# Experts on tokens sorted by expert: ranks and scatters in self-attention, 39 blocks of 256 rows, results scattered back and added

## What is computed

```python
x = x + xattn(layernorm(x), ctx, ctx, mask)       # 128 batches, 32 queries, 257 keys, 16 heads of 8
x = x + attn(layernorm(x), Wq, bq, ..., Wo, bo)   # causal, 32 tokens a batch, log-distance decay
x = x + ffn(layernorm(x), ...)                    # 8 experts, top 2
# ffn, for 4096 tokens xt of 128 channels:
ew, ei = top_k(xt @ gate_w, 2); ew = softmax(ew)
h = gelu(xt @ w1[e] + b1[e])                      # 128 -> 256
o = h @ w2[e] + b2[e]                             # 256 -> 128
y = norm(xt + o) * ln_g[e] + ln_b[e]
out = sum over the two chosen e of ew[e] * y
```

## Time and profile before

| what | value |
|---|---|
| median of 3 runs | 980.72 us |
| profiled execution, its own time | 979.43 us |
| its span, first to last instruction | 977.7 us |
| PE busy | 828.2 us, 85% |
| DVE busy | 829.6 us, 85% |
| ACT busy | 661.4 us, 68% |
| POOL busy | 448.4 us, 46% |
| mean granted TensorE clock | 0.971 of 2.4 GHz |

### The profile page before, as it was taken

The page is one execution under the profiler, slowest core; times in us unless marked ns, Lnnn a source line. Parts: engine busy times, 40 slices in busy tenths (PEclk is TensorE's granted clock), DMA queues, the critical chain, the costliest instruction groups (busy, mean ns, idle before and its releaser), DMA issues. The chain is left out here.

```text
span 977.7 us, 30213 instructions
## 1 busy us (share of the span) xinstructions
PE 828.2 (85%) x9453; PEld 668.0 (68%) x9453; DVE 829.6 (85%) x2343; ACT 661.4 (68%) x2102; POOL 448.4 (46%) x437
## 2 busy tenths in 40 slices
PE   4989889898889988896788888887989889889892
PEld 2666656666666666664678888887888788788782
DVE  4888889888898988986688887874899999999994
ACT  3677777777677777774676666663777677677674
POOL 3222222222222222221454444443677887787785
PEclk9999999999999999999799998999999999999997
DMA  3221111111111111131000000000000000000000
GB/s 85 75 73 49 48 39 49 36 49 48 36 49 41 46 49 38 49 104 61 1 1 0 0 0 0 0 1 1 1 7 11 5 5 11 5 5 11 5 5 17
DMA packets 32695, 27.26 MB, mean 28 GB/s; under 512 B 3548, under 2 KB 32408, under 8 KB 32664
## 3 DMA queue, kind: packets, MB, share of 16 engines
q1 hardware_dynamic: 32664, 26.87, 9.5%
HBM read 24.76 MB, written 2.10 MB: 27 GB/s over the span
## 5 line engine op out<-in xcount | busy, mean ns | idle before, releaser
L545 ACT ACTIVATE E<-SC,neg_max 128x257 f32<-128x257 f32 x512 | 235.9, 474 | 101.7 <-DVE neg_max L605 101.7
L605 DVE TENSOR_REDUCE neg_max<-SC 128x1 f32<-128x257 f32 x512 | 181.9, 418 | 36.4 <-PE SC L402 33.6
L415 PE MATMUL ETP<-ident,E 128*128 128x128 f32 x1024 | 162.8, 287 | 37.7 <-ACT E L545 37.3
L614 DVE TENSOR_TENSOR Et<-ETP,mask_T 128x512 f32<-128x512 f32 x256 | 172.6, 684 | 15.9 <-PE ETP L415 14.8
L415 PEld LDWEIGHTS ETP<-ident,E 128*128 128x128 f32 x1024 | 109.4, 142 | 88.3 <-issue 78.7
L1337 PE MATMUL PO<-W,hid 128*128 128x128 f32 x1024 | 138.1, 278 | 18.8 <-ACT hid L1378 18.8
L1402 ACT ACTIVATE Y<-Z,zb,zs 128x128 f32<-128x128 f32 x256 | 111.0, 485 | 59.9 <-DVE zb L1557 59.9
L1337 PEld LDWEIGHTS PO<-W,hid 128*128 128x128 f32 x1024 | 131.4, 192 | 29.0 <-issue 21.6
L1326 PE MATMUL PH<-xT,W 128*128 128x256 f32 x512 | 135.1, 387 | 0.5 <-ACT xT L1370 0.5
L1378 ACT ACTIVATE hid<-PH,b1c 128x256 f32<-128x256 f32 x256 | 105.5, 463 | 19.4 <-PE PH L1326 17.8
L545 ACT ACTIVATION_READ_ACCUMULATOR E<-SC,neg_max 128x1 f32 x512 | 103.8, 203 | 0.0
(11 more groups left out here) (163 smaller groups left out, 1551.3 us busy)
## 6 DMA issues: line engine op xcount, KB each, us to landing
V<-in_ctx_dram SPq DMA_DIRECT2D x64, 256.0 KB, 2.7
xh<-in_x_dram SPq DMA_DIRECT2D x32, 64.0 KB, 2.2
last_rep<-in_ctx_dram SPq DMA_DIRECT2D x128, 2.0 KB
X<-in_x_dram SPq DMA_DIRECT2D x32, 64.0 KB
out_dram<-Xo SPq DMA_DIRECT2D x64, 32.0 KB, 1.5
W<-in_L_ffn_w_dram SPq DMA_DIRECT2D x1, 1024.0 KB
W<-in_L_ffn_w_dram SPq DMA_DIRECT2D x2, 512.0 KB
b2r<-in_L_ffn_b_dram SPq DMA_DIRECT2D x1, 512.0 KB
```

Source lines behind the costliest of these rows:

```text
L415: i = pe.transpose(ETP[s][:, c:c + P], E[:, j // HB, NQ * (j % HB) + 2 * s + u, k * P:(k + 1) * P], ident[:, :])
L545: i = act.activation(E[:, h, at, :], SC[:, u, 0:S], ACT.Exp, bias=neg_max[:, j % 2, u:u + 1], accum_out=den[:, h, at:at + 1])
L605: dve.tensor_reduce(neg_max[:, j % 2, u:u + 1], SC[:, u, 0:S], AX.X, ALU.max, negate=True).then_inc(max_sb, 1)
L614: dve.tensor_tensor(Et[:, 2 * (j % 2) + s, :, :, :].rearrange("p u k c -> p (u k c)"), ETP[s][:, :], mask_T[:, :, :, :].rearrange("p u k c ...
```

## The change

Stage 1 also fills a DRAM array "slots" (129 slots of 256 rows of 130 words) with empty rows: weight zero, and a destination outside the result. Stage 2 handles, in body t, also tile t-2 for routing: it normalises the new X into XN (written twice, once for each choice, with room for the weight and the destination), and computes the gates. In every second body from the fourth on it chooses two experts for 512 tokens with masks and maxima, ranks the tokens within each expert by products with a triangle and with ones, and gets each row's place in slots, where every expert has room for 16 blocks. POOL scatters the rows by indirect DMAs of 128 rows, 4 for each tile, from body 5 on. The loops of this stage are written out, T + 3 = 19 bodies. At its end DVE lists the blocks in a table: for each of 39, its slot and its expert. Stage 3 runs 39 blocks; SP reads slot and expert from the table and loads rows and first-layer weights; PE, ACT and DVE read the expert into a register each. The weighted result of each block goes by two indirect DMAs to "parts" in DRAM by token and choice; at the end parts is loaded, its two halves and the rest of X are added and stored. All 64 output DMAs now stand behind the last block.

What the diff takes out is the expert stage told above: norm, gates, choice, XB by POOL, the sums on POOL, and the loop constructs of stages 2 and 3.

```diff
--- before.py
+++ after.py
...
+TOKENS = B * L
+ROW = D + 2
+BLK = 256
+NBLK = (2 * TOKENS + NE * (BLK - 1)) // BLK
+NTAB = 40
+PER = TOKENS // BLK
+SPARE = NE * PER
+GB = 4
...
+                def fill(first, n):
+                    sp.dma_start(slots[bass.ds(first, n), :, :].rearrange("n (p e) c -> p n (e c)", e=2),
+                                 empty[:, :, :].rearrange("p e c -> p (e c)").unsqueeze(1).to_broadcast([P, n, 2 * ROW])
+                                 ).then_inc(filled, 16)
...
+                        fill(8 * t, 8)
...
+                fill(8 * (T - 1), 8)
+                fill(0, 8)
+                fill(SPARE, 1)
...
+        PY = ps("PY", [P, 512])
+        RANK = PY[:, 288:288 + (GB + 1) * NE].rearrange("p (g x) -> p g x", x=NE)
...
+                def route_norm(u):
+                    dve.wait_ge(r_rs, u + 1)
+                    xt = tile_of(u)
+                    for e in range(2):
+                        i = dve.tensor_scalar(XN[:, u, e, :, 0:D], xt[:, e * D:(e + 1) * D].unsqueeze(1).to_broadcast([P, 2, D]),
+                                              rmv[:, e, 0:1], rrs[:, e:e + 1], ALU.subtract, ALU.mult)
+                    i.then_inc(r_xn, 1)
...
+                def find_seat(k):
+                    dve.wait_ge(rank_ps, k + 1)
+                    if k > 0:
+                        dve.wait_ge(c_start, k)
+                    dve.tensor_tensor(seat[:, :, :], RANK[:, 0:GB, :], start_of[:, :].unsqueeze(1).to_broadcast([P, GB, NE]),
...
+                    routed = 0 <= u < T
+                    choosing, k = t % 2 == 0 and t >= 4, (t - 4) // 2
+                    if soon:
...
+                        route_var(u)
+                    if choosing:
+                        rank_same(k, 0)
+                    if now:
+                        add_decay(t, 1)
+                    if choosing:
+                        find_lead(k, 0)
+                    if now:
+                        less_maxima(t, 0)
+                    if choosing:
+                        mark(k, 0)
+                    if now:
+                        maxima(t, 1)
+                    if choosing:
+                        leave_out(k)
+                    if now:
+                        sums(t, 0)
+                    if choosing:
+                        find_best(k, 1)
+                    if now:
+                        less_maxima(t, 1)
+                    if choosing:
+                        find_same(k, 1)
+                    if now:
+                        invert(t, 0)
+                    if choosing:
+                        rank_same(k, 1)
+                        find_gap(k)
+                    if routed:
+                        route_norm(u)
+                    if choosing:
+                        find_lead(k, 1)
+                        mark(k, 1)
+                        take(k)
+                    if behind:
                         own(t - 1, 0)
+                    if routed:
+                        keep_gates(u)
+                    if behind:
                         own(t - 1, 1)
+                    if soon:
                         norm(t + 2)
+                    if choosing:
+                        add_one(k)
+                        find_seat(k)
+                    if now:
+                        sums(t, 1)
+                    if choosing:
+                        move_start(k)
+                        first_share(k)
+                        own_seats(k)
+                    if now:
+                        invert(t, 1)
+                    if choosing:
+                        second_share(k)
+                        find_place(k)
+                    if behind:
                         add(t - 1)
+                    if choosing:
+                        send_share(k)
+                        keep_place(k)
+                        part(k)
+                        keep_weights(k)
                 for t in range(2):
                     norm_stats(t)
                     norm_mean(t)
                     norm_var(t)
                     norm(t)
+                dve.memset(wt[:, :, :], 0.0)
+                for t in range(T + 3):
+                    body(t)
...
+                def send(v):
+                    pool.wait_ge(placed, v // 2 + 1)
+                    pool.wait_ge(c_sent_w, v // 2 + 1)
+                    for e in range(2):
+                        for c in range(2):
+                            pool.indirect_dma_start(slots.rearrange("n r c -> (n r) c"),
+                                                    bass.IndirectOffsetOnAxis(ap=place_i[:, v, e, c:c + 1], axis=0),
+                                                    XN[:, v, e, c, :], None).then_inc(sent, 16)
...
+                    if 0 <= t - 2 < T:
+                        route_power(t - 2)
+                    if t + 1 < T:
                         front(t + 1)
+                    if t < T:
+                        normalise(t, 0)
+                        normalise(t, 1)
+                    if t >= 5:
+                        send(t - 5)
...
+                def route_turn(u):
+                    pe.wait_ge(r_xn, u + 1)
+                    for e in range(2):
+                        i = pe.transpose(PY[:, e * P:(e + 1) * P], XN[:, u, e, 0, 0:D], ident[:, :])
...
+                def ranks(k):
+                    pe.wait_ge(c_taken, k + 1)
+                    pe.wait_ge(g_sb, min(2 * k + 3, T))
+                    pe.matmul(RANK[:, 0, :], before_me[:, :], taken[:, 0, :], start=True, stop=True)
+                    for g in range(GB):
+                        pe.matmul(RANK[:, g + 1:GB + 1, :], all_ones[:, :], taken[:, g, :].unsqueeze(1).to_broadcast([P, GB - g, NE]),
+                                  start=(g == 0), stop=False, skip_group_check=True)
+                    pe.matmul(RANK[:, 1:GB, :], before_me[:, :], taken[:, 1:GB, :], start=False, stop=True,
...
+                    if now:
+                        scores(t, 1)
+                    if behind:
                         turn_probs(t - 1, 1)
+                    if soon:
                         project(t + 1)
+                    if now:
+                        values(t, 0)
+                    if routed:
+                        route_turn(u)
+                    if behind:
                         weigh(t - 1, 0)
+                    if routed:
+                        route_gates(u)
+                    if behind:
                         weigh(t - 1, 1)
+                    if t % 2 == 0 and t >= 4:
+                        ranks((t - 4) // 2)
+                    if now:
+                        values(t, 1)
+                    if behind:
                         project_out(t - 1)
...
+            def load_weights(i):
+                if i >= NW:
+                    sp.wait_ge(h_ps, FH * (i - NW + 1))
+                    sp.nop(nofuse=True)
+                e = sp.value_load(table[0:1, 1, i:i + 1], min_val=0, max_val=NE - 1)
+                sp.dma_start(W1[:, i % NW, :], w1[bass.ds(e, 1), :, :].rearrange("e c f -> c (e f)")).then_inc(w1_in[i % NW], 16)
+            load_weights(0)
+            sp.wait_ge(sent, 16 * 4 * T)
+            for i in range(NBLK):
+                if i >= NX:
+                    wait_gone(sp, i - NX)
+                    sp.nop(nofuse=True)
+                n = sp.value_load(table[0:1, 0, i:i + 1], min_val=0, max_val=SPARE)
+                sp.dma_start(XS[:, i % NX, :, :].rearrange("p e c -> p (e c)"),
+                             slots[bass.ds(n, 1), :, :].rearrange("n (p e) c -> p (n e c)", e=2)).then_inc(xs_in[i % NX], 16)
+                if i + 1 < NBLK:
+                    load_weights(i + 1)
+            for i in range(NBLK - NX, NBLK):
+                wait_gone(sp, i)
+            for c in range(T // 2):
+                for k in range(2):
+                    sp.dma_start(YB[:, k, 2 * c:2 * c + 2, :],
+                                 parts[TOKENS * k + 4 * P * c:TOKENS * k + 4 * P * (c + 1), :].rearrange(
+                                     "(t p e) d -> p t (e d)", t=2, p=P)).then_inc(y_in[c], 16)
...
+            for t in range(T):
                 sp.wait_ge(x3, t + 1)
                 for q in range(HQ):
+                    sp.dma_start(out[TB * t:TB * t + TB, :, :].rearrange("b (g q e) c -> q b g (e c)", g=NQ, q=HQ)[q],
+                                 YB[32 * q:32 * q + 32, 0, t, :]).then_inc(stored, 16)
...
+                    pool.wait_ge(z_s, i - 1)
+                pool.tensor_tensor(zr[:, i % 2, :], zv[:, i % 2, :], neg_half[:, 0:2], ALU.pow).then_inc(z_r, 1)
+            def send(i):
+                pool.wait_ge(u_sb, i + 1)
+                for e in range(2):
+                    pool.indirect_dma_start(parts, bass.IndirectOffsetOnAxis(
+                        ap=XS[:, i % NX, e, D + 1:D + 2].bitcast(I32), axis=0), YO[:, i % NY, e, :], None,
+                        bounds_check=2 * TOKENS - 1, oob_is_err=False).then_inc(gone[i % NX], 16)
```

(70 more changed lines are left out.)

935 lines of the change are left out of this document (448 added, 487 removed).

## The result

The changed kernel takes 1054.83 us (median of four runs, 1053.85 to 1056.14) where the kernel before took 981.37 beside it: ratio 1.0745, interval 1.072 to 1.077, 7.4% slower. The forecast was 974 us, 928 to 1040. The profiled execution has a span of 1052.1 us.

A forecast was written before the change was run, and what follows sets the result against it. It took PE and DVE as near full in the experts and a DVE-PE-DVE ring as binding self-attention. Scatters landing at 772 us, first block 779, 38 steps to 927, end to 972.2, plus 1.7 gave 974 us, range 928 to 1040.

The forecast's parts named there:

- Then PE in series: ... 16.6 us: Self-attention body without choice: from decay add, XN ready at 8.05 us, then PE's transposes to scores in series, 16.6 us.
- The mean is 17.6: Self-attention bodies 4 to 15: mean of 16.6 us without and 18.6 with a choice, 211 us for twelve.
- handovers 0.4: Self-attention body: 0.4 us in PE's series for all passing of work between engines.
- The choice: Every second self-attention body: 0.5 us from VectorE's small operations and 1.5 from ranks on PE, 18.6 us a body.
- the held subtraction: Self-attention: DVE's subtraction takes 2.80 us beside POOL's Qbd product; about 1.0 of the choice's 1.5 us falls there.
- POOL ... hidden: Self-attention: POOL's work with powers and four scatters a tile, 11.4 of 17.6 us, adds nothing to the body.
- Some 10 us less: Whole kernel: with about 1 us for an indirect DMA instead of 1.2, the sum would fall some 10 us.
- The register read: Expert blocks: PE, ACT and DVE each read the expert's number into a register, taken as 0.8 us.
- the ring: Expert blocks: DVE variance, POOL power, DVE factors, register read and statistics to the next variance set 3.9 us a block.
- POOL as the bound by a slow DMA: Expert blocks and self-attention: an indirect DMA of 2.1 us makes POOL the bound, blocks 5.0 us, kernel 1030; 28%.
- Routing hidden: Self-attention: routing work fits in DVE's held time, bodies 15.5 us, 28 us less, kernel 946; 24% with its variants.
- Rival 1: Expert blocks and self-attention: POOL becomes the bound through indirect DMAs of 2.1 us, kernel 1030; 28%.

The follow-up runs named there:

- run 10: Kernel with route products a body later, ScalarE's copy early and scatters between normalisations, plus each choice's second half (ranks, seats, places, weights) moved to the next body: 929.46 us.
- run 4: Changed kernel with 14 unused products of constant matrices on TensorE in each body 2 to 15, where it waits for XN: 1044.78 us.
- run 7: Changed kernel with route products a body later, ScalarE's copy ahead of the second exponentials, and scatters between GpSimd's two normalisations: 953.64 us.
- run 3: Changed kernel with each row scatter of tiles 0 to 13 issued once more, into a table nobody reads: 1106.02 us.
- run 2: Changed kernel with route transposes, ScalarE's copy and gates a body later, choice in odd bodies, scatters one body later: 996.89 us.
- run 1: Changed kernel with TensorE's route products behind both weighings and VectorE's copy of the gates behind the second own heads: 987.39 us.

## Why the prediction was wrong

Where the sum stood and what came (us of the span):

| step | forecast | measured |
|---|---|---|
| cross-attention, bodies 0 and 1 | 494.6 | 492.7 |
| bodies 2 and 3 | 33 | 39.9 |
| bodies 4 to 15 | 211 | 282.9 |
| body 16, to its addition | 12 | 17.6 |
| last routing and choice | 9.7 | 11.5 |
| last scatters, to the output of the first block's second layer | 18.3 | 29.3 |
| other 38 blocks | 148 | 124.1 |
| last block, to its last scatter landed | 7.6 | 13.2 |
| end | 37.6 | 40.9 |

(492.7 is the first addition at 491.6 and 1.1 us to the decay add; the last choice is done at 844.6, VectorE takes up the output of the first block's second layer at 873.9 and the last one's at 998.0, and the first load of the end begins at 1011.2.)

**The step that failed** is "Then PE in series: ... 16.6 us" and with it "The mean is 17.6": 21.4 was measured in a body without a choice and 23.6 in the mean, 72 us over twelve bodies. The order was right to the operation. XN was forecast to end at 8.05 us after the decay add and ended at 8.35 (654.67 to 663.02). Behind it the series was priced with rows of a TensorE at full clock, and the change itself takes that away: TensorE stands 5.4 to 7.5 us in each of the bodies 4 to 14 ahead of that series. At half clock the two weighings, values and transposes took 6.6 us for 3.4, and the gates 1.02 for 0.51: 3.7 us of the 4.8 that such a body was too long. The unforeseen wait below is the other term; the two sum to a little more than 4.8, as the products' starts overlap. The sign stood in the prediction's own rows: in the kernel before, TensorE waits 2.06 us for the projection, and the scores behind it take 1.61 us, against 1.06 for the other half's at 603.90. The forecast used that slow rate for half of the scores alone. The Trainium skill (TensorE: Matmul & The Clock Gate, Part 1: The HAM clock gate) says that the array's clock is set by how busy it has been; the trace agrees, with 0.69 in this stage and 0.93 in run 10, where the same products stand without the wait for XN. What a body would take with this order at full clock stays open: run 4 raised the clock only to 0.79, and what followed its wait still ran at 0.50.

**A wait that was not in the sum** is the 1.95 us ahead of the gates. The prediction counted "handovers 0.4". ScalarE's copy of the turned rows stands behind values(t, 0), which waits for the first weighing (ACT L1339 on L1449, 46.2 us), and so the gates wait for a weighing that they have nothing to do with. Every queue that a moved step passes had to be read; ScalarE's was not.

**The choice** was forecast at 2.0 us more for such a body and cost 4.9 (26.3 against 21.4). The ranks took 2.4 us from start to values, not 1.5 (half clock again), the projection 3.44 instead of 2.52 (body 10 against body 9), and XN came 1.9 us later after the decay add, behind nine small operations that were only partly in the shadow of the held subtraction. In run 7 a body with a choice was still 5.3 us longer than one without, in run 10 at most 2.8.

**"POOL ... hidden"** held only just. An indirect DMA takes 0.96 us and 0.30 to the next, 1.26 for a forecast of 1.2. But the share of 11.4 us in 17.6 was the wrong measure: run 3 shows that what stands behind the scatters, the powers, has a time at which it is due: of 5.05 us more, only about 1 was hidden. ("Some 10 us less" for scatters of 1 us is also wrong: with GpSimd hidden, only the last 8 scatters and the last block's two are in the sum, which is 2 us.)

**Right:** the fills (0), and the 64 stores at 0.47 us alone at the end. The register read was near, 0.59 for 0.8. The Trainium skill (DMA: Bandwidth & Descriptors, Latency and other measured facts) puts a register's load at about 0.6 us at least, and VectorE's 0.59 agrees. **Near by luck:** the block stages. A block took 3.27 us by 3.9, 24 us less over 38, and the ring was not what set it but GpSimd's power and scatters. Against that stand 11 us more ahead of the blocks (the rows are asked for 7.7 us after the last scatter's issue, the first products again run at half rate, and ScalarE loads a table for 1.28 us) and 6 us more behind the last, where GpSimd's scatters had queued up.

**The rivals.** POOL as the bound by a slow DMA (2.1 us, 1030) fell in its price: a scatter takes 1.26. Its sign, GpSimd without idle time in the expert stage, is there all the same, because the ring came out shorter than forecast. The Trainium skill's rule that a 2-port operation of VectorE starves descriptor building (SBUF — State Buffer, Who interferes with whom) isn't seen: the 64 scatters of rows took 0.96 to 1.22 us, the 78 of results 0.97 to 1.17. The reverse is seen: VectorE's variance takes 0.30 us beside them for 0.17. Routing hidden (946) fell for the kernel as it stands, though run 7 reached 954 with another order. Rival 1 had the right sign by the wrong mechanism, and no rival had the clock, so that the range ended at 1040.

## What to carry to other kernels

Work added to a ring is priced by what stands behind it in each in-order queue, not by the engines' shares: here 62 us more of VectorE's busy time cost 195, and with the same operations a body later, the copy early, the scatters in a gap and the ranks spread over two bodies, about 70. If a step makes TensorE wait some microseconds in every turn, price what follows at half clock too, and look in the old trace for products that already slow down behind a wait. Move the consumer until its input is old, look which wait has taken its place, and repeat; the first such move (run 2) looked worse than a cruder one (run 1) only because one copy stood in the wrong place.

## What the runs showed of the hardware

What is held beside GpSimd's Qbd product (2.34 us) is not the long subtraction as such. In run 10 a copy of 8 columns fell there in its place, took 2.13 us where it takes 0.17 elsewhere (L1058 at 653.39 in the changed kernel), and the subtraction behind it took 0.68. Timelines of VectorE and GpSimd:

```profile
642.17 2.13 DVE L1058 COPY XN<-share 128x8 f32<-128x8 f32 x1
644.22 0.68 DVE L937 TENSOR_TENSOR E<-E,mx 128x512 f32<-128x512 f32 x1
```

```profile
641.92 2.34 POOL L1236 TENSOR_TENSOR Qbd<-Qt,hh_scaled 128x1024 f32<-128x1024 f32 x1 [0.96 <-ACT Qt L1330]
```

A reduction was not held. This one began 0.13 us after the same Qbd product and took 0.21 us, as it did away from it (696.75 in the changed kernel):

```profile
642.05 0.21 DVE L1087 TENSOR_REDUCE place<-seats 128x8 f32<-128x64 f32 x1
```

So which operation falls beside Qbd decides, and a small copy moved there costs two microseconds (here it only took the subtraction's turn). An indirect DMA of GpSimd holds VectorE too: the variance of a block (2 columns, L1788) took a median of 0.30 us in the changed kernel, ending with the scatter, and 0.17 without one.
